# Another order of ScalarE's and VectorE's work in the encoder attention, and the loops over pairs of tiles unrolled

## The reference

```python
# layer 0: 8 heads, exp(-(a_s - a_n)^2) masked by adj > 0, rows divided by their sum
x = _layernorm(x + layer0(x, adj))
# layer 1: adj @ (x @ W), 8 heads
x = _layernorm(x + layer1(x, adj))
# layer 2: masked softmax of leaky(s1[:, None] + s2[None, :]), times x @ fc_w
x = _layernorm(x + layer2(x, adj))
# layer 3: encoder and decoder; 4 heads of 128
Xw = jnp.einsum('hnd,hde->hne', Xh, W)
sig = jax.nn.sigmoid(f1[:, :, None] + f2[:, None, :])
att = _masked_softmax(adj[None] * sig, (adj != 0)[None])
Xc = (att @ Xw)                      # the encoder attention
emb = mlp_block(batchnorm(Xc))
out = mlp_block(elu((att @ emb) @ W^T))
x = _layernorm(x + out)
```

## Time and profile before

| | |
|---|---|
| time, median of 3 runs | 3706.84 us (3699.71 to 3708.7) |
| the profiled execution | 3702.97 us, its span 3701.1 us |
| TensorE busy | 3251.3 us, 88% of the span, 13231 matmuls |
| VectorE busy | 2320.1 us, 63% |
| ScalarE busy | 1633.0 us, 44% |
| GpSimd busy | 238.1 us, 6% |
| mean granted TensorE clock | 0.963 of full speed |

### The profile page before, as it was taken

One profiled execution on the slowest core, in us unless ns is written; L12 is line 12 of the kernel. 1 busy time (PEld: TensorE's weight loads), 2 busy tenths in 40 slices (PEclk: granted clock), 3 DMA queues, 4 the chain that ended last, 5 costly groups with the idle time before them and its releaser, 6 DMA issues. The chain is left out here.

```text
span 3701.1 us, 38125 instructions
## 1 busy us (share of the span) xinstructions
PE 3251.3 (88%) x13231; PEld 2093.6 (57%) x13231; DVE 2320.1 (63%) x3048; ACT 1633.0 (44%) x1399; POOL 238.1 (6%) x397
## 2 busy tenths in 40 slices
PE   5799999999977899995999995999999966999995
PEld 4533333333322677773454444777777835888884
DVE  5589888988865466655666554777777744122226
ACT  0288888888832111112222215787777602000002
POOL 0000000000001011110000001000000000000003
PEclk9999999999999899997999997999999988999997
DMA  7500000000013465652222216666566631876654
GB/s 278 196 16 8 16 8 15 15 8 14 7 62 106 168 250 224 240 218 109 97 96 96 96 63 243 240 239 258 225 259 233 240 105 69 356 275 262 265 221 125
DMA packets 109980, 557.02 MB, mean 151 GB/s; under 512 B 12576, under 2 KB 20995, under 8 KB 86064
## 3 DMA queue, kind: packets, MB, share of 16 engines
q1 hardware_dynamic: 90800, 431.91, 30.8%
q0 software_dynamic: 19072, 123.65, 9.2%
HBM read 363.33 MB, written 192.18 MB: 150 GB/s over the span
## 5 line engine op out<-in xcount | busy, mean ns | idle before, releaser
L518 PE MATMUL bank<-dist,hf 128*65 128x512 f32 (+2 forms) x2112 | 830.4, 546 | 64.2 <-ACT dist L480 64.2
L518 PEld LDWEIGHTS bank<-dist,hf 128*65 128x65 f32 x2112 | 277.1, 138 | 609.6 <-issue 457.1
L1345 PE MATMUL bank<-pt,HA 128*128 128x256 f32 x1936 | 504.3, 380 | 3.0 <-DMA HA<-features 3.0
L480 ACT ACTIVATE dist<-dist 128x1408 f32<-128x1408 f32 (+1 forms) x352 | 453.8, 1324 | 1.4
L985 PE MATMUL bank<-HB,pt 128*128 128x512 f32 x968 | 438.4, 594 | 0.0
L1534 PE MATMUL bank<-w,EM 128*128 128x256 f32 x1936 | 426.1, 380 | 12.2 <-DMA w<-weights 12.2
L1534 PEld LDWEIGHTS bank<-w,EM 128*128 128x128 f32 x1936 | 369.0, 191 | 62.9 <-DMA w<-weights 12.4
L1333 PE MATMUL bank<-idt,v 128*128 128x128 f32 x1936 | 304.3, 278 | 78.3 <-ACT pt L1223 50.7
L411 DVE TENSOR_TENSOR dist<-msk,sB 128x1408 f32<-128x1408 uint8 (+1 forms) x208 | 325.6, 1565 | 74.1 <-PE bank L518 65.4
L471 ACT ACTIVATE dist<-dist,neg_t 128x1408 f32<-128x1408 f32 (+1 forms) x208 | 296.3, 1424 | 145.1 <-DVE dist L411 145.1
L1345 PEld LDWEIGHTS bank<-pt,HA 128*128 128x128 f32 x1936 | 328.2, 191 | 26.7 <-DMA HA<-features 3.4
(11 more groups left out here) (153 smaller groups left out, 3707.6 us busy)
## 6 DMA issues: line engine op xcount, KB each, us to landing
w<-weights SPq DMA_DIRECT2D x44, 2816.0 KB, 9.8
weights<-pt SPq DMA_DIRECT2D x220, 512.0 KB, 3.6
al<-in_adj_cols SPq DMA_DIRECT2D x22, 1408.0 KB, 8.2
at<-in_adj_tiles SPq DMA_DIRECT2D x22, 1408.0 KB, 8.2
rows<-in_adj_rows SPq DMA_DIRECT2D x22, 1408.0 KB, 6.8
mrow<-in_adj_rows POOLq DMA_DIRECT2D x22, 1354.0 KB, 6.9
rows_low<-mrow POOLq DMA_DIRECT2D x22, 1354.0 KB, 6.0
rows<-rows_low POOLq DMA_DIRECT2D x22, 1354.0 KB, 8.5
```

The source lines that it names most:

```text
L480: act.activation(d[:, 0:VALID[c]], d[:, 0:VALID[c]], ACT.Exp, scale=-1.0).then_inc(p_ready, 1)
L518: mm = pe.matmul(sums_bank(hh, k)[0:FW, 0:hi - a * P], hf[hh][:, m, :], d[:, a * P:hi], start=(m == 0), stop=(m == T - 1))
L1345: t = pe.matmul(acc_t[n % 2][:, 0:P2], HA[:, m, h * D3:(h + 1) * D3], pt[n % 2][:, m, :, :].rearrange("p r n -> p (r n)"), start=(m == 0), ...
```

## The change

Two edits. `pair_loop` runs the body with plain numbers all 11 times, so every wait is on a constant. In the encoder attention ScalarE scores a batch in the order 0, 3, 1, 2 (SCORE_ORDER), and its copies stand at other places; VectorE weighs unit u+3 after group WEIGH_AT[u % 4] instead of always after the fifth (index 4), and waits for the sigmoid by its place in the new order. No instruction's work is changed, and the table loads stay two to a batch.

```diff
+SCORE_ORDER = (0, 3, 1, 2)
+WEIGH_AT = (1, 4, 3, 3)
...
 def pair_loop(eng, body, first=0, last=False):
 
-    lo, hi = int(first), PAIRS - int(last)
-    for i in range(lo):
+    for i in range(PAIRS):
         body(i)
-    with eng.Fori(lo, hi) as i:
-        body(i)
-    if last:
-        body(PAIRS - 1)
...
-                        if u < 8 and r == 0:
+                        if u < 8:
                             act.wait_ge(fb_in[h], 16)
...
-                    for u in range(4):
-                        score(u)
+                    for k in SCORE_ORDER:
+                        score(k)
                     for b in range(0, UNITS, 4):
                         more = b + 4 < UNITS
                         expo(b)
-                        if b > 0:
-                            keep(b - 1)
                         expo(b + 1)
                         expo(b + 2)
                         keep(b)
                         expo(b + 3)
                         if more:
-                            score(b + 4)
+                            score(b + SCORE_ORDER[0] + 4)
+                            score(b + SCORE_ORDER[1] + 4)
                         keep(b + 1)
                         if more:
-                            score(b + 5)
+                            score(b + SCORE_ORDER[2] + 4)
                         if b % 8 == 0 and b > 0:
                             ri_out(b // 8 - 1)
-                        if more:
-                            score(b + 6)
                         keep(b + 2)
                         if more:
-                            score(b + 7)
-                    keep(UNITS - 1)
+                            score(b + SCORE_ORDER[3] + 4)
+                        keep(b + 3)
                     ri_out(PAIRS - 1)
...
-                        dve.wait_ge(sig_ready, u + 1)
+                        dve.wait_ge(sig_ready, u // 4 * 4 + SCORE_ORDER.index(u % 4) + 1)
...
-                            if g == 4 and u + 3 < UNITS:
+                            if g == WEIGH_AT[u % 4] and u + 3 < UNITS:
                                 weigh(u + 3)
```

## The result

| | before | after |
|---|---|---|
| median of the runs | 3707.77 us (4 runs, 3699.71 to 3715.16) | 3665.21 us (4 runs, 3654.76 to 3666.43) |
| ratio after / before | | 0.9881, 95% interval 0.9864 to 0.9898 |
| profiled execution, its span | 3702.97, 3701.1 us | 3664.09, 3662.3 us |

The change is faster by 43 us. I had forecast 75 (3632 us), and 3665 lies above the range of 3614 to 3658. The direction was right, the size was not.

A forecast was written before the change was run, and what follows sets the result against it. TensorE was taken to bound the encoder attention; 3703 less 49 (attention) and 24 (constants) gave 3630, plus half of the 3.9 us by which the profiled execution lay below the median: 3632 us, range 3614 to 3658.

The forecast's parts named there:

- steps 1 to 4: Encoder attention: reordered weighing, copies and sigmoids cut a batch from 31.62 to about 29.25 us, 49 us over 21 batches.
- step 1: Encoder attention: weighing of unit b+3 moves to after unit b's second group, so its exponential starts 3.38 us earlier.
- Attention, the start: Encoder attention's start: later first exponentials cost nothing, hidden by TensorE's wait for the features' load; 2.5 us without that cover.
- the failed term: Adjacency stage: constant waits shorten a round from 20.06 to 19.4 us, saving 12 us, bounds 0 to 14.
- Graph attention: Graph attention stage: constants save three hops, 0.27 us a tile, 5 us in all, bounds 0 to 5.
- Projection: Projection after layer 0: constants save three hops in 20 tiles, 5 us, between 0 and 7.
- Preparation: Preparation, 20 to 150 us: the same hops beside busy transfers save 2 us, between 0 and 3.
- B: Constant waits: register work hides in waits, transfers carry the round; a quarter of 24 us kept, 3650 us, chance 0.12.
- C: Encoder attention: inverse of the sums stands behind the moved weighing on VectorE, a new wait; 3662 us, chance 0.08.
- D: Encoder attention: a switch costs a second table load after a waiting copy, 1.28 us more; 3683 us, chance 0.01.
- E: Unrolled stages: straight-line code not fetched in time, 186 us if fully exposed; 3818 us, chance 0.03.
- the signs: Attention: right if copy waits under 10 us, maximum under 1; wrong if copy of b+1 waits above 0.5 a batch.

The follow-up runs named there:

- the pair of runs: Changed kernel with the store of mrow on SyncE's queue directly ahead of the load of at, 3626.55 us, or directly behind it, 3776.54 us.
- second median: The changed kernel measured again, as it is, beside later edits: 3651.95 us over six runs, ratio 0.9849.

## Why the prediction was wrong

*Attention, steps 1 to 4: right.* Copy of b+1, copy of b+2, copy of b+3 and the exponential moved as laid out; 29.22 us was measured where nothing else interfered, 29.25 forecast. Table switches cost what the row said: 1.28 us plus 0.02 (2490.10 to 2491.40). The 1380 ns of drain that the Trainium skill (ScalarE: Activation LUTs) adds are not in this trace, and the batch followed the row.

*Attention, the size of step 1.* "The moved weighing runs from T+2.7 to T+5.7" counted 2.97 us for it. It starts at T+2.6 and takes 3.69 us whenever GpSimd's product of the pair before is still running. Nine batches lose 0.7 to 1.0 us by it, 7 in all; with the product one unit later the loss is gone, in four kernels. I had looked at what stands behind the weighing on VectorE, not at what runs beside it on GpSimd. The Trainium skill (SBUF — State Buffer, SBUF: two separate sides) has the rule: of a VectorE operation with two SBUF inputs and a GpSimd operation that reads SBUF, whichever starts first holds a shared pair of ports for its whole length and the other is blocked. The trace agrees: 0.84 us of overlap, 0.72 longer; 1.13 us of overlap, 1.00 longer; and the product itself, which starts first, keeps its 2.39 us.

*Attention, the start.* "I cost at nothing ... without that cover it is 2.5 us." The cover was not there: 2.2 us. The wait for the features is ScalarE's own, and the new order puts two sigmoids behind it. The first batch saved 0.7 us instead of 2.35.

*Adjacency stage: the failed term.* "A round takes 20.06 us and holds two issues, so 19.4 after. Saved 12" took the landings as fixed while the hops around them shrank. Neither landing is fixed. The reload of `mrow` lands later: in quiet stretches (no slow round) a round has 0.77 us less of hops (0.68 to 0.31 at the store, 0.68 to 0.28 at the reload), but the reload lands after 7.3 to 7.5 us for 6.9, and the round takes 19.8 us for 20.0 (25 rounds of three unrolled traces, 14 of the trace before). The store is the worse one: it is 6.4 or 10.6 us by whether it is issued before the load of `at`. An estimate from these figures: 21 rounds with 0.2 us less are 5 us gained, three slow rounds more at 7 us are 21 lost, together 16 for the 14.8 measured. In the looped kernel's quiet stretch the store goes mostly 1.1 to 1.5 us ahead; unrolled it goes 0.7 to 1.1 ahead, and passes the edge near 0.5 in two to four of 21 rounds. That the narrower margin is why slow rounds are more common is argued from these rows; that the order sets the landing is shown by the pair of runs. Also wrong was the lower bound of 0: a loss was not excluded by any reason.

*Graph attention:* mis-sized. "5 us, which is also the upper bound" counted three hops; 9.7 was measured. The hops gave 0.24 us a tile, 5 us as counted; the other 5 are the irregular waits, gone too, and that part is luck. Why they were there was not tried. *Projection:* 4.1 for 5. *Preparation:* 0.4 to 0.8 for 2.

*The rivals.* B (transfers carry the round, which stays near 20) is nearest for the quiet rounds; it had no loss in it. C did not come: the inverse of the sums made no gap. D did not come: the table loads stay at 1.28 us, two to a batch. E did not come: 28 packets more and no unnamed wait of TensorE. Of the signs, the wait for ScalarE's copy (12.5 us, under 10 was right) and the wait for the maximum (0.38 and 1.11 us by turns, under 1 was right) half held, and the 0.68 us for the copy of b+1, in every second batch, is near the sign that step 1 was too small.

*The range.* It held the change's second median (3652) and not its first (3665). A stage whose time changed by 20 us with the fall of a few rounds could have been seen in the trace before: its second store waited 11.6 us, all others about 6.7.

## What to carry to other kernels

When a change shortens hops, ask which order of two DMAs on different queues was kept only by the old delays; fix that order in the program (one queue, store first if something waits for it) before counting the gain. Where an instruction is moved, look at what the other engines run at the new place, as GpSimd's product here beside VectorE's weighing. A wait seen on a queue need not belong to the work behind it: an operation that depends on nothing there should stand ahead of it, except where that delays the last load of the stage.

## What the runs showed of the hardware that I had not expected

- A store of 1.35 MB and a load of 1.4 MB issued within 1 to 2 us of each other do not share evenly. On one queue, store first: store 5.7 and load 7.9 us to landing (medians); load first: load 7.3 and store 10.3. With the store on GpSimd's queue the edge lies where it is 0.4 to 0.6 us ahead, in the ten executions counted; on SyncE's queue 0.36 us ahead was still quick. A store 3.5 us and more behind the load was quick again (5.5 to 6.2 us). What in the DMA engines does it was not tried.
- VectorE's weighing took 2.97 us alone, and 3.69 and 3.97 where it began 0.84 and 1.13 us before the end of GpSimd's product.
- Waits against registers lengthen each hop (0.66 for 0.31 us to an issue, 0.13 for 0.03 after the power), and yet 22 tiles of such a stage took 427.4 us with them and 427.7 without, where TensorE set the pace.
- A wait of TensorE of 6.5 us is paid a second time: it lasted from 1335.1 to 1341.65 us, the granted clock was 0.50 (the level of 1.2 GHz) from 1337.5 to 1347.0, and four transposes took 1.12 us for 0.66. The trace before shows the same behind its one slow round (0.50 from 1277.5 to 1287.0).
